# Top-2 mixture of a fused AdaLN-FFN kernel: dense experts with gates, against tiles of scattered token rows with weights at register addresses

## The chip, the cores and the metric

One core of one Trainium2 chip. The metric is device time in microseconds for one execution; lower is better. Three runs of the kernel before gave a median of 1235.52 us (1235.36 to 1236.33).

## The reference, cut to what matters

Two layers on x of 16 x 256 tokens with 256 features (4096 tokens). Layer 0 is a recurrence over 256 steps, then a top-2 mixture of 8 large experts, added to x. Layer 1 conditions x with a shared gated MLP plus a second top-2 mixture of 8 small experts, feeds the result through a quantised FFN and adds it to x. The change touches the second mixture:

```python
def _L1_cond_ref(x, t_emb, router_w, router_t_w, router_bias, sw1, sw3, sw2, rw1, rw2):
    shared_out = jnp.einsum('nh,dh->nd', jax.nn.silu(x_flat @ sw1.T) * (x_flat @ sw3.T), sw2)
    s = jax.nn.sigmoid((x_flat @ router_w.T + t_bias_flat).astype(jnp.float32))
    _, topk_idx = jax.lax.top_k(s + router_bias, TOP_K)
    s_sel = jnp.take_along_axis(s, topk_idx, axis=1)
    gates = jnp.where(denom > EPS, s_sel / (denom + EPS), 1.0 / TOP_K)
    combine = jnp.sum(gates[:, :, None] * jax.nn.one_hot(topk_idx, N_EXPERTS), axis=1)
    H = jax.nn.gelu(jnp.einsum('nd,ehd->enh', x_flat, rw1), approximate=False)   # h = 128
    O = jnp.einsum('enh,edh->end', H, rw2)
    out = (shared_out + jnp.einsum('end,ne->nd', O, combine)) / (N_SHARED + TOP_K)
```

The reference computes all 8 experts for every token and zeroes six of them by `combine`. The FFN behind it needs the largest value of the whole mixture output before it can quantise anything.

## The kernel before, in words

The program runs four stages one behind the other: the recurrence (its token rows are scattered to expert rooms in HBM while it runs), the large experts (39 tiles of 256 token rows, `experts_*`), the mixture (`mixture_pe`, `mixture_act`, `mixture_dve`) and the quantised FFN (`ffn_*`). Each engine has its own instruction stream in a fixed order written out by hand; semaphores tie the streams together. Each fp32 product is made of three f16 products (high by high, high by low, low by high), `split_matmul` (L570 to L573).

The large experts end with scattered adds of their result tiles into `results` in HBM (`store_results`, L1298, from POOL). SyncE then loads `results` back as x1, 512 KB for each group of 512 tokens (`load_x1`, L1467).

The mixture works on 8 groups of 4 x 128 tokens. For a group, ScalarE makes the high half of x (`input_hi`, L668), VectorE the low half (`input_lo`, L734), TensorE transposes both (L605) and ScalarE copies them out of PSUM (`input_T`, L672). TensorE then computes router logits (24 small matmuls), the first layer of the shared MLP (8 units of 6 matmuls with 512 columns), **the first layer of all 8 routed experts** (8 more units like these), the shared second layer (4 units of 12 matmuls with 256 columns) and **the second layer of all 8 experts** (16 units of 2 x 3 matmuls with 256 columns). ScalarE applies tanh or gelu; VectorE finishes the SiLU product (L763, L767), makes low halves (L756), runs the top-2 routing as a chain of small operations (L793 to L807, L775 to L788) and adds each expert's part with its gate as a per-token factor (L836). After each group VectorE takes the largest value (L847, L842); the FFN starts when the last is in (L992).

POOL does nothing in the mixture; its indirect DMAs are in the recurrence (L1268, one row of 1028 bytes for each of 128 partitions, plain write) and in the large experts (L1298, 1024 bytes for each, added to what stands in HBM).

```python
for q2 in range(0, GT, 2):                       # L836, dense: every expert's part of every token
    ...
    dve.scalar_tensor_tensor(y[:, GT * g + q], ps[:, bank_of(...), j * D:(j + 1) * D],
                             comb[:, q, 2 * p + j:2 * p + j + 1], y[:, GT * g + q], ALU.mult, ALU.add)
```

Of the kernel before, what the change touches and what calls it, by code (L numbers as in the profile page):

```python
# [17 lines left out]
P = 128  # L18
# [51 lines left out]
HC = HSC + E  # L70
U_SHARED, U_ROUTED = 1, 1 + 2 * HSC
U_NEXT = U_ROUTED + E
U_OUT = U_NEXT + DC
U_PAIR = U_OUT + GT
UNITS = U_PAIR + GT * E // 2
PRE_UNITS = 1 + DC
YG = GT * (1 + E)
MIX_SCALE = W_SCALE * A_SCALE
LINKS = 24
# [16 lines left out]
def build_program(nc, zT, xn, h0T, WT, b_row, alphaT, gate_wT, gate_b, w1T, b1T, w2T, b2, rwT, rtwT, rbias,  # L96
                  sw1T, sw3T, sw2T, rw1T, rw2T, fw1n, fb1T, fw2n, fb2, const, rows_d, results_d, out):
    ctx = ExitStack()
    with ctx:
# [18 lines left out]
        def carve(a):  # L118
# [3 lines left out]
            def part(n, dt=F32):  # L122
# [10 lines left out]
        hid1_flat = part(2 * HC * GN, F16)  # L133
        hid1 = hid1_flat.rearrange("p (s c n) -> p s c n", s=2, c=HC)
        yqT = hid1_flat[:, 0:DC * N].bitcast(BF16).rearrange("p (k n) -> p k n", k=DC)
        vq_flat = hid1_flat[:, DC * N:].bitcast(U8)
# [3 lines left out]
        xs_flat = part(2 * 2 * DC * GN, F16)  # L140
        xs = xs_flat.rearrange("p (b s k n) -> p b s k n", b=2, s=2, k=DC)
        xsn_flat = part(2 * GT * D, F16)
        xsn = xsn_flat.rearrange("p (s n) -> p s n", s=2)
# [3 lines left out]
        diag = part(DC * P).rearrange("p (c n) -> p c n", c=DC)  # L147
        h0rep = part(DC * P).rearrange("p (c n) -> p c n", c=DC)
        rs2 = part(D)
# [5 lines left out]
        l1w = part(2 * 7168, F16).rearrange("p (s n) -> p s n", s=2)  # L155
        sw1s = l1w[:, :, 0:1024].rearrange("p s (k h) -> p s k h", k=DC)
        sw3s = l1w[:, :, 1024:2048].rearrange("p s (k h) -> p s k h", k=DC)
        sw2s = l1w[:, :, 2048:3072].rearrange("p s (k d) -> p s k d", k=HSC)
        rw1s = l1w[:, :, 3072:5120].rearrange("p s (k h) -> p s k h", k=DC)
        rw2s = l1w[:, :, 5120:7168].rearrange("p s (e d) -> p s e d", e=E)  # L160
        wq_n = part(2 * 2048, BF16).rearrange("p (m n) -> p m n", m=2)
# [29 lines left out]
              for a in (hid.rearrange("p s f n -> p (s f n)"), xs_flat)]  # L191
# [130 lines left out]
        xn_lo = sem("xn_lo")  # L322
        xs_T = sem("xs_T")
        unit = sem("unit")
        sa_used = sem("sa_used")
        tb_ready = sem("tb_ready")
        router_step = sem("router_step")
        ymax_in = sem("ymax_in")
# [1462 lines left out]
```

## Time and profile before

| | us |
|---|---|
| median of three runs | 1235.52 |
| the profiled execution | 1231.89 |
| its span | 1229.8 |
| TensorE busy | 1102.4 (90%) |
| VectorE busy | 898.7 (73%) |
| ScalarE busy | 550.1 (45%) |
| POOL busy | 246.3 (20%) |

The profiled execution is 2.1 us longer than its span (what lies before the first and behind the last instruction) and 3.6 us shorter than the median of the other runs. In the chain that ended last the share of TensorE is 77%, VectorE 10%, ScalarE 8%.

### The profile page before, as it was taken

How to read it: one execution, taken by the hardware profiler on the slowest of the kernel's cores; microseconds unless marked ns; L12 is line 12 of the kernel's file. 1: busy time of each engine (PE TensorE's matmuls, PEld its weight loads, DVE VectorE, ACT ScalarE, POOL GpSimd, SP SyncE). 2: the span in 40 equal slices, each digit the busy share in tenths (PEclk: the TensorE clock that was granted, in tenths of full speed). 3: DMA queues.
4: the chain of work that ended last, by engine and by line, in shares of the span. 5: the costliest groups of instructions: out<-in, count | busy, mean ns of one | idle time of the engine just before them, and what ended most of it. 6: DMA issues, size and time to landing. Idle time of an engine off the chain costs nothing.

```text
span 1229.8 us, 31887 instructions
## 1 busy us (share of the span) xinstructions
PE 1102.4 (90%) x10420; PEld 847.4 (69%) x10421; DVE 898.7 (73%) x3007; ACT 550.1 (45%) x1743; POOL 246.3 (20%) x285
## 2 busy tenths in 40 slices
PE   6777777877878999999999999789999999996898
PEld 5665665665657888888888888646776567763355
DVE  5676676776776688965555555468898988988887
ACT  4555555555554333333333333362445424444276
POOL 1002112112115675243333333300000000001000
PEclk9999999999999999999999999989999999998999
DMA  7222332332334577444444444241000000000024
GB/s 179 78 71 86 100 94 85 100 98 81 99 96 113 94 168 141 88 73 61 63 62 63 64 64 64 50 124 69 2 1 1 0 1 1 1 1 1 1 34 105
DMA packets 98711, 82.31 MB, mean 67 GB/s; under 512 B 58529, under 2 KB 88354, under 8 KB 98594
## 3 DMA queue, kind: packets, MB, share of 16 engines
q1 hardware_dynamic: 82946, 57.98, 18.6%
q0 software_dynamic: 15648, 22.86, 10.7%
q8 instruction: 62, 1.02, 0.3%
q14 instruction: 55, 0.45, 0.1%
HBM read 41.18 MB, written 33.60 MB: 61 GB/s over the span
## 4 chain that ended last, share of the span: by engine, by line
PE 77%; DVE 10%; ACT 8%; issue 3%; DMA 1%; SPq 0%; POOL 0%; DVEq 0%
PE ps L572 24%; PE ps L1129 17%; PE ps L1139 17%; PE ps L1686 7%; DVE ps L1615 6%; PE ps L1691 4%; ACT work L1539 4%; ACT ps L1534 3%; DVE imax L1008 2%; PE ps L1656 2%; PE ps L917 1%; PE ps L922 1%; PE ps L888 1%; PE ps L1664 1%; DVE W L836 1%
## 5 line engine op out<-in xcount | busy, mean ns | idle before, releaser
L1157 ACT ACTIVATE lane<-ps,b_now 128x256 f32<-128x256 f32 x312 | 147.7, 474 | 260.0 <-PE ps L1129 246.0
L1129 PE MATMUL ps<-lane,W 128*128 128x256 f16 x1872 | 212.8, 274 | 0.9 <-issue 0.8
L1139 PE MATMUL ps<-W,lane 128*128 x1872 | 210.9, 273 | 0.2
L1129 PEld LDWEIGHTS ps<-lane,W 128*128 x1872 | 183.7, 98 | 23.8 <-issue 1.7
L1139 PEld LDWEIGHTS ps<-W,lane 128*128 128x128 f16 x1872 | 182.6, 98 | 22.3 <-issue 0.8
L1686 PE MATMUL ps<-work 128*128 128x16 f16 x2048 | 98.9, 177 | 86.1 <-ACT work L1539 85.5
L1686 PEld LDWEIGHTS ps<-work 128*128 128x128 f16 x2048 | 76.2, 107 | 137.8 <-ACT work L1539 136.4
L572 PE MATMUL ps<-W,work 128*128 128x512 f16 x768 | 168.5, 381 | 0.1
L1298 POOL DMA_INDIRECT results<-lane,dest x78 | 124.7, 1598 | 217.0 <-DVE lane L1212 184.3
L1224 DVE TENSOR_TENSOR lane<-lane 128x256 f16<-128x256 f32 x312 | 133.3, 427 | 10.8
L572 PEld LDWEIGHTS ps<-W,work 128*128 128x128 f16 x768 | 74.8, 98 | 90.1 <-issue 1.9
L572 PE MATMUL ps<-work,W 128*128 128x256 f16 x1152 | 127.4, 273 | 0.0
L572 PEld LDWEIGHTS ps<-work,W 128*128 128x128 f16 x1152 | 112.2, 98 | 13.7 <-ACT W L672 0.6
L1222 DVE CAST lane<-lane 128x256 f16<-128x256 f32 x312 | 92.8, 298 | 20.6 <-ACT lane L1157 20.6
L1212 DVE SCALAR_TENSOR_TENSOR lane<-ps,b_now 128x512 f32<-128x512 f32 x39 | 26.9, 691 | 110.7 <-PE ps L1139 110.7
L1629 DVE TENSOR_TENSOR work<-ps,work 128x32 f16<-128x32 f32 x256 | 48.9, 191 | 78.4 <-ACT ps L1541 78.1
L1656 PE MATMUL ps<-work 128*128 128x128 f32 x256 | 98.3, 490 | 5.8 <-DVE work L1579 4.9
L836 DVE SCALAR_TENSOR_TENSOR W<-ps,comb,W 128x256 f32 (+1 forms) x256 | 101.6, 474 | 2.0 <-PE ps L572 1.9
L1615 DVE TENSOR_TENSOR_SCAN ps<-ps,work 128x64 f32<-128x64 f32 x256 | 76.4, 298 | 30.9 <-ACT ps L1534 8.2
L1268 POOL DMA_INDIRECT rows<-work,slot_of x64 | 63.1, 985 | 156.5 <-DVE ps L1615 152.6
L1598 DVE SCALAR_TENSOR_TENSOR work<-ps,alpha,work 128x16 f32<-128x16 f32 x510 | 93.3, 225 | 0.0
L1534 ACT ACTIVATE ps<-ps 128x32 f32<-128x32 f32 x256 | 46.6, 182 | 94.8 <-PE ps L1691 94.8
(213 smaller groups left out, 1466.7 us busy)
## 6 DMA issues: line engine op xcount, KB each, us to landing
stage<-in_w1T SPq DMA_DIRECT2D x16, 512.0 KB, 3.6
stage<-in_w2T SPq DMA_DIRECT2D x16, 512.0 KB, 4.1
b_now<-in_b SPq DMA_DIRECT2D x39, 128.0 KB
work<-in_zT SPq DMA_DIRECT2D x32, 128.0 KB, 2.1
results<-in_xn SPq DMA_DIRECT2D x32, 128.0 KB
W<-results SPq DMA_DIRECT2D x8, 512.0 KB, 3.8
rows<-work SPq DMA_DIRECT2D x8, 257.0 KB, 5.2
out<-W SPq DMA_DIRECT2D x4, 512.0 KB, 4.0
```

What stands on the lines that cost most here:

```text
L572: last = pe.matmul(dst, lhs(a, k), rhs(b, k), start=(n == 0 and k == ks[0]), stop=(n == 2 and k == ks[-1]))
L836: dve.scalar_tensor_tensor(y[:, GT * g + q], ps[:, bank_of(U_PAIR + GT * p + q), j * D:(j + 1) * D], comb[:, q, 2 * p + j:2 * p + j + 1], ...
L1129: last = pe.matmul(ps[:, f % 4, 0:ST], of_e(W1[:, bass.ds(e, 1), a, k, f * P:(f + 1) * P]), xT[:, p, b, k], start=(i == 0 and k == 0), sto ...
L1139: last = pe.matmul(ps[:, 4 + q, 0:D], hid[:, a, f, q * P:(q + 1) * P], of_e(W2[:, bass.ds(e, 1), b, f]), start=(i == 0 and f == 0), stop=( ...
L1157: act.activation(v4[:, f % 4], ps[:, f % 4, 0:ST], ACT.Relu, bias=b1_now[:, p, f:f + 1], scale=A_SCALE / W_SCALE).then_inc(l1_v, 1)
L1222: dve.tensor_copy(hid[:, 0, f], v4[:, f % 4]).then_inc(split0, 1)
L1224: dve.tensor_tensor(hid[:, 1, f], v4[:, f % 4], hid[:, 0, f], ALU.subtract).then_inc(l1_hid, 1)
L1298: pool.indirect_dma_start(out=results_d, in_=obuf[:, p, q], in_offset=None, compute_op=ALU.add, out_offset=bass.IndirectOffsetOnAxis(ap=de ...
L1598: dve.scalar_tensor_tensor(zs[:, j % 2, c // BATCH, k, :, 1], h[:, k], alpha[:, k:k + 1], z[:, j, k, c:c + BATCH], ALU.mult, ALU.add).then ...
L1615: dve.tensor_tensor_scan(ps[:, 5, 0:2 * DB], ps[:, 6, 0:2 * DB], zs[:, j % 2, s % STEPS_PER_TILE].rearrange("p c b v -> p (c b v)"), 0.0, ...
L1656: pe.matmul(dst, wz[:, k, cols], z[:, slot, k, :], start=(k == 0), stop=False, skip_group_check=True)
L1686: pe.matmul(ps[:, b + m, c:c + BATCH], w[:, k, m * P:(m + 1) * P], hring[:, prev, 0, k, pc:pc + BATCH], start=False, stop=False, skip_grou ...
```

## The change

The routed experts of the second mixture are no longer computed for all tokens. In order:

- **Routing and scatter.** Two groups are routed at once (`PAIR` = 8 tiles of 128 tokens, 32 chained operations, `mix_route_op`), in 4 steps. TensorE counts ranks (`mix_ranks`) so that every token gets a slot in a room of its expert. POOL scatters each group's rows (high and low halves of x, token number and gates: `MROW` = 260 words, 1040 bytes) to `mrows` in HBM, 8 indirect DMAs a group, 64 in all (`mixture_pool`). The rows wait in 4 buffers (`XBUFS`). While this runs, TensorE and VectorE work on the shared MLP, 8 units a step (32 of 96), and 12 units more after the last step.
- **Table.** VectorE makes a table of 39 tiles of 256 slots (`mix_table`), SyncE writes padding behind every expert's last row and loads the tiles, 3 buffers (`TILE_BUFS`).
- **Tiles.** For each of 39 tiles: TensorE transposes it (8 transposes), 6 matmuls of 256 columns, gelu, high and low halves, 6 matmuls of 256 columns; both layers read the expert's weights at an address from a register. VectorE multiplies by the gate (`tile_out`) into `mout`, and POOL scatters the tile's two halves, plain writes of 1024 bytes a row, to `mresults` in HBM at `mdest`. 30 shared units are spread over the tiles; 22 follow.
- **Combine.** When the last tile has landed, SyncE loads `mresults` (1 MB a group, two results a token); VectorE adds them to the shared part and takes the group's largest value.

PSUM: the units have 3 banks in turn where they had 8. At the start 8 unused rooms of `mrows` are filled from an input (2.1 MB, HBM to HBM). Cut to its core:

```diff
+TAIL = 4
+MROW = D + TAIL
+XBUFS = 4
+PAIR = 2 * GT
+STEPS_M = GROUPS // 2
+TILE_BUFS = 3
+MIX_OPS = 32
+UNITS = 2 * HSC + GT
+STEP_UNITS = 8
+BRIDGE_UNITS = 12
+TILE_UNITS = 30
+LATE = 6
+COMBINE = (0, 1, 2, 6, 3, 4, 5, 7)
...
         def mixture_act(act):
             def input_hi(g):
...
+                if g >= XBUFS:
+                    act.wait_ge(moved[b], 2 * GT * 16 * (g // XBUFS))
+                act.activation(xsn[:, b, :, 0:D], x1[:, GT * g:GT * g + GT], ACT.Copy, scale=A_SCALE).then_inc(xn_hi, 1)
...
+            def tile_gates(n):
+                b = n % TILE_BUFS
+                tail = lambda k: mrow[:, b, :, D + k:D + k + 1]
+                mine = mtile_f[:, 0, n]
+                dve.wait_ge(mrow_in[b], 16 * (n // TILE_BUFS) + 16)
+                if n >= TILE_BUFS:
+                    dve.wait_ge(mstored[b], SQ * 16 * (n // TILE_BUFS))
+                dve.scalar_tensor_tensor(mdest[:, b], tail(1), mine, tail(0), ALU.is_equal, ALU.add).then_inc(mdest_set, 1)
+                dve.scalar_tensor_tensor(mmask[:, b], tail(1), mine, tail(3), ALU.is_equal, ALU.mult).then_inc(mgate_step, 1)
+                dve.wait_ge(mgate_step, 2 * n + 1)
+                dve.tensor_tensor(mgate[:, b], mmask[:, b], tail(2), ALU.add).then_inc(mgate_step, 1)
...
+            for n in range(SLOT_TILES):
+                tile_lo(n)
+                for v in tile_units(n):
+                    shared(v)
+                if n < SLOT_TILES - 1:
+                    tile_gates(n + 1)
+                if n:
+                    tile_out(n - 1)
+            tile_out(SLOT_TILES - 1)
+
+            def combine(at):
+                g, b = COMBINE[at], at % TILE_BUFS
+                yg = y[:, GT * g:GT * g + GT]
+                if g < LATE:
+                    dve.wait_ge(routed_in[b], 16 * (at // TILE_BUFS) + 16)
+                    link(dve, dve.tensor_tensor(yg, yg, routed[b][:, :, 0], ALU.add))
+                else:
+                    dve.wait_ge(unit_read, output_unit(g, GT - 1) + 1)
+                link(dve, dve.tensor_tensor(yg, yg, routed[b][:, :, 1], ALU.add))
+                dve.tensor_reduce(ymax[:, g:g + 1], yg.rearrange("p q d -> p (q d)"), AX.X, ALU.max).then_inc(combined, 1)
...
+        def mixture_pool(pool):
+            rows_flat = mrows_d.rearrange("r s n -> (r s) n")
+            for g in range(GROUPS):
+                pool.wait_ge(router_step, MIX_OPS * (g // 2 + 1))
+                pool.wait_ge(xn_lo, g + 1)
+                pool.wait_ge(tok_set, g + 1)
+                for k in range(2):
+                    for q in range(GT):
+                        at = GT * (g % XBUFS) + q
+                        pool.indirect_dma_start(out=rows_flat, in_=xrow[:, g % XBUFS, q], in_offset=None,
+                                                out_offset=bass.IndirectOffsetOnAxis(ap=mslot_of[:, k, at:at + 1], axis=0))\
+                            .then_inc(moved[g % XBUFS], 16)
+            for n in range(SLOT_TILES):
+                b = n % TILE_BUFS
+                pool.wait_ge(mout_set, n + 1)
+                pool.wait_ge(mdest_set, n + 1)
+                for q in range(SQ):
+                    pool.indirect_dma_start(out=mresults_d, in_=mout[:, b, q], in_offset=None,
+                                            out_offset=bass.IndirectOffsetOnAxis(ap=mdest[:, b, q], axis=0))\
+                        .then_inc(mstored[b], 16)
```

The last combines stand on VectorE as follows: 8 units, combine 0 to 2, the 4 output units of group 6, combine 3, then three times 2 units and a combine (4, 5, 6), the 4 output units of group 7, combine 7.

The order of VectorE's work in the tile stage of the change, tiles 4 and 5 of the loop; `mdest`, `mmask` and `mgate` are the three operations of `tile_gates` (L1039 to L1042), L1053 is `tile_out`, L1046 `tile_lo`, L985 the read of a shared output unit:

```order
L1053 TENSOR_TENSOR lane<-ps,mgate 128x512 [waits mgate_step,m2_ps]
L1046 SCALAR_TENSOR_TENSOR lane<-work,lane 128x256 [waits mhi]
L985 TENSOR_SCALAR W<-ps 128x256 [waits unit]
L1039 SCALAR_TENSOR_TENSOR mdest<-stage,mtile_f 128x2 [waits mstored1,mrow_in1]
L1040 SCALAR_TENSOR_TENSOR mmask<-stage,mtile_f 128x2
L1042 TENSOR_TENSOR mgate<-mmask,stage 128x2 [waits mgate_step]
L1053 TENSOR_TENSOR lane<-ps,mgate 128x512 [waits mgate_step,m2_ps]
L1046 SCALAR_TENSOR_TENSOR lane<-work,lane 128x256 [waits mhi]
L1039 SCALAR_TENSOR_TENSOR mdest<-stage,mtile_f 128x2 [waits mstored2,mrow_in2]
```

Here the wait for a tile's scattered results (`mstored`) stands between one `tile_out` and the next; before the change VectorE waited in this stage for TensorE, ScalarE and itself.

POOL's queue in the change, from the last row scatter to the first result scatters:

```order
L1328 DMA mrows<-W,mslot_of 36864x260 [waits tok_set,xn_lo,router_step]
L1328 DMA mrows<-W,mslot_of 36864x260 x7
L1336 DMA mresults<-lane,mdest 16384x256 [waits mdest_set,mout_set]
L1336 DMA mresults<-lane,mdest 16384x256
L1336 DMA mresults<-lane,mdest 16384x256 [waits mdest_set,mout_set]
```

Before the change POOL's queue goes from its last L1298 straight to the FFN's work; 64 + 78 indirect DMAs now stand between.

## Rows read from the trace of the kernel before

**Rows 1.** The page: span, and the chain that ended last by line.

```profile
span 1229.8 us, 31887 instructions
...
PE ps L572 24%; PE ps L1129 17%; PE ps L1139 17%; PE ps L1686 7%; DVE ps L1615 6%; PE ps L1691 4%; ACT work L1539 4%; ACT ps L1534 3%; DVE imax L1008 2%; PE ps L1656 2%; PE ps L917 1%; PE ps L922 1%; PE ps L888 1%; PE ps L1664 1%; DVE W L836 1%
```

**Rows 2.** Busy time by stage: the mixture and its first 10 us.

```profile
795.00:1115.00 320.00, 307.21 (x2241) 200.97 (x2242) 270.83 (x666) 132.54 (x227) 0.64 (x2) 0.98 0.07 21
...
795.00:805.00 10.00, 2.23 (x23) 1.74 (x23) 1.23 (x1) 4.28 (x5) 0.64 (x2) 0.66 0.42 117
```

**Rows 3.** The chain of waits in the mixture: start, us, what.

```profile
904.53 37.04 PE ps L572 x264
...
959.03 20.89 PE ps L572 x96
...
1113.69 0.70 DVE ymax L842
```

**Rows 4.** The timeline of the mixture: start, us, engine, line.

```profile
800.23 1.06 ACT L668 ACTIVATE W<-W 128x1024 f16<-128x1024 f32 x1 [4.04 <-DMA W<-results]
...
801.34 1.03 PE L605 MATMUL ps<-identh,W 128*128 128x128 f16 x8 [7.68 <-ACT W L668]
...
804.84 0.78 PE L572 MATMUL ps<-rw_s,W 128*128 128x8 f16 x24 [1.21 <-ACT W L672]
...
805.66 0.19 DVE L793 SCALAR_TENSOR_TENSOR r_sel<-ps,t_bias 128x32 f32<-128x32 f32 x1 [3.12 <-PE ps L572]
...
1093.95 15.88 PE L572 MATMUL ps<-work,W 128*128 128x256 f16 x144
```

**Rows 5.** Groups of instructions by line and form: busy, mean ns | idle before.

```profile
L1157 ACT ACTIVATE lane<-ps,b_now 128x256 f32<-128x256 f32 x312 | 147.7, 474 | 260.0 <-PE ps L1129 246.0 <-DVE lane L1224 9.1 <-issue 0.3
L1224 DVE TENSOR_TENSOR lane<-lane 128x256 f16<-128x256 f32 x312 | 133.3, 427 | 10.8
L836 DVE SCALAR_TENSOR_TENSOR W<-ps,comb,W 128x256 f32 x192 | 76.1, 473 | 1.2 <-PE ps L572 1.1
L767 DVE SCALAR_TENSOR_TENSOR W<-ps,W 128x512 f32<-128x512 f32 x32 | 22.1, 691 | 3.3
L672 ACT ACTIVATE W<-ps 128x1024 f16<-128x1024 f16 x16 | 15.5, 1019 | 1.4 <-PE ps L605 1.4
L825 DVE TENSOR_SCALAR W<-ps 128x256 f32 x24 | 8.6, 414 | 0.8 <-PE ps L572 0.8
L1045 DVE TENSOR_TENSOR W<-W 128x1024 f32<-128x1024 f32 x4 | 4.6, 1216 | 0.0
L803 DVE TENSOR_TENSOR r_t<-r_t,prio 128x32 f32<-128x32 f32 x16 | 3.1, 192 | 0.5
L779 DVE TENSOR_SCALAR r_k<-r_m 128x4 f32<-128x4 f32 x8 | 1.3, 162 | 0.0
L710 ACT ACT_TABLE_LOAD x1 | 1.3, 1283 | 0.0
```

**Rows 6.** The timeline of POOL: scattered rows one behind the other.

```profile
381.07 0.96 POOL L1268 DMA_INDIRECT rows<-work,slot_of  x1 [0.30 <-issue]
382.34 0.97 POOL L1268 DMA_INDIRECT rows<-work,slot_of  x1 [0.30 <-issue]
```

**Rows 7.** L1268 asked for by line: from its start to its landing.

```profile
DMA to landing us min/median/max: 2.4/3.0/4.5
```

**Rows 8.** The timeline around the last results of the large experts.

```profile
779.55 0.69 DVE L1212 SCALAR_TENSOR_TENSOR lane<-ps,b_now 128x512 f32<-128x512 f32 x1 [3.56 <-PE ps L1139]
...
780.52 1.55 POOL L1298 DMA_INDIRECT results<-lane,dest  x1 [6.29 <-DVE lane L1212]
...
782.38 1.55 POOL L1298 DMA_INDIRECT results<-lane,dest  x1 [0.30 <-issue]
...
792.86 1.55 POOL L1298 DMA_INDIRECT results<-lane,dest  x1 [0.30 <-issue]
...
796.52 8.51 SPq L1467 DMA_DIRECT2D W<-results  x3
```

**Rows 9.** DMA issues: KB each, median us to landing.

```profile
W<-results SPq DMA_DIRECT2D x8, 512.0 KB, 3.8
```

More of the change, by code:

```diff
@@ new lines, in router @@
+            def router(g):
+                pe.wait_ge(xs_T, 2 * g + 2)
+                if g >= 2 and g % 2 == 0:
+                    pe.wait_ge(router_step, MIX_OPS * (g // 2 - 1) + 1)
+                for q in range(GT):
+                    at = (GT * (g % 2) + q) * E
+                    last = split_matmul(ps[:, 2, at:at + E], lambda s, k: xs[:, g, s, k, q * P:(q + 1) * P],
+                                        lambda s, k: rw_s[:, s, k], range(DC))
+                last.then_inc(rt_ps, 1)
@@ new lines, in mix_ranks @@
+            def mix_ranks(m):
+                flat = m16_m[:].rearrange("p j e -> p (j e)")
+                pe.wait_ge(router_step, MIX_OPS * m + 15)
+                pe.matmul(MIX_RANKS, tri[:], flat, start=True, stop=False, skip_group_check=True)
+                for j in range(PAIR):
+                    last = pe.matmul(MIX_RANKS[:, (j + 1) * E:], ones16[:],
+                                     m16_m[:, j:j + 1].broadcast_to([P, PAIR - j, E]),
+                                     start=False, stop=(j == PAIR - 1), skip_group_check=True)
+                last.then_inc(rank_ps, 1)
@@ L663, in mixture_pe @@
-            mix_groups(pe, mix)
+            for g in range(2):
+                transposes(g)
+            pe.wait_ge(tb_ready, 1)
+            pe.wait_ge(wt_cp, 4)
+            pe.wait_ge(m16_zero, 1)
+            for m in range(STEPS_M):
+                v = STEP_UNITS * m
+                for g in (2 * m, 2 * m + 1):
+                    router(g)
+                for k in range(3):
+                    shared(v + k)
+                mix_ranks(m)
+                for k in range(3, 6):
+                    shared(v + k)
+                for g in (2 * m + 2, 2 * m + 3):
+                    if g < GROUPS:
+                        transposes(g)
+                    shared(v + 4 + g - 2 * m)
@@ new lines, in mixture_pe @@
+            pe.wait_ge(mtable, 1)
+            tile_transposes(0)
+            ex = None
+            for n in range(SLOT_TILES):
+                if n < SLOT_TILES - 1:
+                    tile_transposes(n + 1)
+                ahead = tile_first(n)
+                for v in tile_units(n):
+                    shared(v)
+                if n:
+                    tile_second(n - 1, ex)
+                ex = ahead
+            tile_second(SLOT_TILES - 1, ex)
+            for v in range(TAIL_UNIT, UNITS * GROUPS):
+                shared(v)
@@ new lines, in mixture_dve @@
+            first_late, last_late = output_unit(LATE, 0), output_unit(GROUPS - 1, 0)
+            for v in range(TAIL_UNIT, first_late):
+                shared(v)
+            for at in range(3):
+                combine(at)
+            for v in range(first_late, first_late + GT):
+                shared(v)
+            combine(3)
+            for n in range(3):
+                for v in range(first_late + GT + 2 * n, first_late + GT + 2 * n + 2):
+                    shared(v)
+                combine(4 + n)
@@ L853, in ffn_groups @@
+            for v in range(last_late, UNITS * GROUPS):
+                shared(v)
+            combine(GROUPS - 1)
         def ffn_groups(eng, group):
@@ L1513, in _ @@
             experts_pool(pool)
+            mixture_pool(pool)
             ffn_pool(pool)
```

751 lines of the change are left out of this document (460 added, 291 removed).

## The prediction

> **What bounds the kernel now.** I read the page first: one TensorE line, L572, carries 24% of the chain that ended last [rows 1]. It is the mixture's matmul helper, so the mixture is the largest piece of the path after the two layers of the large experts. The stage table then says how: in 320 us of mixture TensorE is busy 307.2, VectorE 270.8, ScalarE 132.5 and POOL 0.6 [rows 2]. The chain of waits shows nothing but TensorE for whole groups: 37.04 us for 264 matmuls [rows 3], plus 0.9 us of transposes. So the mixture is bound by TensorE, with VectorE some 12% behind it, and POOL and the DMA (7% busy) stand free. The piece ends with the last maximum at 1113.69 + 0.70 = 1114.4 [rows 3]; the 115.4 us behind it are the FFN, which the change leaves alone.
>
> **What the change takes off TensorE.** A 512-column matmul costs 20.89 / 96 = 0.218 us [rows 3], one of 256 columns 15.88 / 144 = 0.110 [rows 4]. Per group the routed experts lose 48 x 0.218 + 96 x 0.110 = 21.0 us of the 37.9, 168 us over 8 groups. Each of 39 tiles adds 12 x 0.110 and 8 transposes of 0.056 (half the 1.03 us of eight at the lower clock [rows 4]), 1.77 us, 69 us in all. TensorE's work falls by 99 us. If TensorE stayed the bound, that would be the gain. I think it does not stay the bound, and go through the new path piece by piece.
>
> **1. To the first slots.** x1 lands at 800.23 and VectorE reads the first logits at 805.66 [rows 4]. Now two groups have to be transposed and routed first: two more ScalarE copies of 1.02 [rows 5] and 24 more router matmuls, 0.78 [rows 4]: 808.4. Then 31 chained operations. Small ones take 0.16 to 0.19 [rows 5]; with the handover and a few twice as wide I take 0.21, 6.5 us. Five unit operations of 0.69 stand between them, 3.4, and about 3 us go into the first unit and its tanh. The slots stand at 821.3.
>
> **2. 64 row scatters on POOL.** The nearest row is L1268, a plain scatter of 1028 bytes a partition: its starts are 382.34 - 381.07 = 1.27 us apart when nothing holds it [rows 6], the landing is 3.0 us from the start (2.4 to 4.5) [rows 7]. I take 1.26: 63 x 1.26 + 3.0 = 82.4, from 821.3 to 903.7. Meanwhile VectorE needs per step 32 x 0.21 + 3 x 3 x 0.69 + 4 x 0.41 + 2 x 1.22 = 17 us [rows 5], under POOL's 16 x 1.26 = 20.2, and TensorE about 14. So this stretch is POOL's, and the shared units, the table and the bridge units are hidden in it (all done near 900). The four row buffers bite: group 7 can only be rounded once group 3 has landed, about 864, its slots come near 880, and POOL wants them at 882. The cover is 2 us thin; if it is gone, a few us are lost.
>
> **3. First tile.** A tile is 266 KB; 512 KB land in 3.8 us [rows 9], I take 3.2. Then transposes, copy 1.02, transposes and first layer 1.1, the one table load of gelu 1.28, gelu 0.47, halves 0.8, second layer 0.66, `tile_out` 0.69 [rows 5] and handovers of 0.2 each: 8.2. First `tile_out` done: 915.1.
>
> **4. The tile loop.** This term decides. In VectorE's order the wait for `mstored` of tile n - 3 stands directly ahead of `tile_out` of tile n - 2. So every `tile_out` from tile 1 on waits until the results of the tile just before it have landed in HBM. The three buffers overlap nothing: `mdest` is rewritten two tiles too early. One round is: `tile_out` to POOL's start 0.28 (779.55 + 0.69 to 780.52) [rows 8]; the second scatter starts 1.26 later [rows 6] and lands 3.0 after that [rows 7]; three small operations 0.16 each with one handover, 0.55; `tile_out` 0.69 plus 0.03 [rows 5, 8]. **5.81 us a tile.** TensorE wants 1.77 + 0.77 units of 1.31 = 2.8, ScalarE 1.02 + 0.47 + 0.4 + 0.3 = 2.2, VectorE 2.3: all wait. There are 36 such rounds (tiles 1 to 36): 209.2 us, to 1124.3.
>
> What bounds it: a landing of 2.4 gives 5.21 [rows 7]. If the plain scatter costs what the adding one does (starts 1.86 apart; the last starts at 792.86 and SyncE goes on at 796.52, 3.6 later [rows 8]) a round is 7.0. The new scatter is plain and as wide as L1268, so I stay with 5.81. The Trainium skill (DMA: Bandwidth & Descriptors, Anatomy of one DMA) puts a DMA issued from POOL at about 2.0 us plus bytes / 436e3, an estimate of 2.3 us for these 131 KB. By it a round would be 5.1 and the sum 25 us lower; the trace's 3.0 disagrees and is used.
>
> **5. Landing the last three tiles.** They follow each other on POOL: 0.28 + 5 x 1.26 + 3.0 = 9.6, to 1133.9. Eight shared units fit beside it.
>
> **6. Loading and combining.** 1 MB: between 3.8 and twice that [rows 9]; I take 5.4: 1139.3. Then VectorE: two adds and a maximum of 1024 values, 1.22 each [rows 5], for six groups 22.0; one add and a maximum for two, 4.9; 8 output units of 0.47 [rows 5], 3.8; three pairs of first-layer units, 9 x 0.69 = 6.2. Group 7's output units need a low half that VectorE makes only then, so TensorE's 4 x 1.31 is exposed, +4.7. Together 41.6, loads hidden behind it from the second on. End 1180.9.
>
> **Sum.** The mixture ends at 1180.9 where it ended at 1114.4: **+66.5 us**. On the profiled execution that is 1231.89 + 66.5 = 1298.4; its like of the median, 3.6 higher, is 1235.52 + 66.5 = **1302.0**. Free of cost I count the 2.1 MB copy at the start: the recurrence waits for other engines and not for DMA after its first 10 us; bound +3 us.
>
> **Rivals.**
> - *The tile loop runs at TensorE's pace.* If the stores came back within the 2.8 us that TensorE needs, 36 x 3.0 = 108 us would fall away: 1194, faster than before. The point at which it decides: the round must be under 5.81 - 66.5 / 36 = 3.96 us. For it speaks that the DMA is idle here. Against: without any landing time, 0.28 + 1.26 + 0.96 + 0.55 + 0.72 = 3.77 us stand in the round already, so the landing would have to follow POOL within 0.2 us, and the shortest of 64 was 2.4 - 0.96 = 1.4 us behind it [rows 6, 7]. It could only be that the order is not what I read. 4%.
> - *The plain result scatter is as dear as the adding one.* 36 x 1.17 + 3.6 = +46 us: 1348. For it: the same 1024 bytes from the same kind of tile; against: L1268 differs from it by 4 bytes a row and writes plainly too. 10%.
> - *TensorE falls to its lower clock in the loop.* In the first 10 us of the mixture, after 7.7 us of idling, the granted clock was 0.66, and eight transposes took 1.03 us [rows 2, 4]. In the loop TensorE would work 2.8 us and idle 3.0. At 1.2 GHz a tile is 5.6 us of work, still under 5.81, but its handovers (some 0.9) are then in the way: 6.5 a round, +25 us, 1327. 14%. The Trainium skill (TensorE: Matmul & The Clock Gate, HAM oscillation — how this bites in real kernels) tells of just this, bursts shorter than the waits between them, with every burst starting at the lower clock; it is the rule that speaks against this change, and rows of a 320 us stage at 0.98 cannot show it.
> - *Landings are quick.* 2.4 us everywhere: 36 x 0.6 and some, 1278. It is the low side of the forecast.
>
> **How the numbers follow.** Forecast with both its sides 72%, higher rivals 24%, the faster one 4%. The range runs from the quick landing with 10 us off my estimated terms (1278 - 13 = 1265) to the dear scatter (1348): 1265 to 1348. A measurement here tells about 0.2%, 2.5 us, from no change. No case lands near zero: slower 0.95, same 0.01, faster 0.04.
>
> **What would show it.** In the profile after: POOL's L1328 64 times, 1.26 apart, nearly without gaps; VectorE's longest wait in total at L1039, released by the DMA to `mresults`, about 3.3 us for each of 36; L1053 every 5.8 us; TensorE about half busy between 915 and 1124. If L1039 waits little and L1053 stands 2.8 to 3 us apart, step 4 is wrong and the kernel is faster. If the rounds are 5.8 but the end is not near 1298, steps 1 to 3 or 6 are.

## The result and the profile after

| | before | changed |
|---|---|---|
| median of four runs, us | 1235.92 (1235.36 to 1236.65) | 1340.49 (1338.51 to 1343.26) |
| ratio | | 1.0847, 95% interval 1.0826 to 1.0869 |
| profiled execution, its span | | 1341.17, 1339.3 |

The change makes the kernel 8.5% slower (4.7% when the same kernel ran again, run 9 below); the forecast was 1302.0 with a range of 1265 to 1348. The direction is right and the time lies inside the range, 38.5 us above the forecast. As it turns out below, two terms missed in opposite directions, and the larger miss is not a property of the code alone.

The page of the changed kernel, its head and the chain that ended last (against [rows 1]):

```profile
span 1339.3 us, 31036 instructions
PE 1071.3 (80%) x10084; PEld 812.9 (61%) x10085; DVE 823.0 (61%) x2840; ACT 552.0 (41%) x1736; POOL 388.2 (29%) x428
PE 51%; issue 15%; DVE 15%; ACT 8%; POOL 5%; another core or an unknown queue 3%; DMA 2%; SPq 0%; DVEq 0%; POOLq 0%; ACTq 0%
```

TensorE's share of the chain fell from 77% to 51%. Its busy time fell by 31 us and not by the 99 that I counted, mostly since it worked at a lower clock: in the whole mixture stage it is busy for 275.2 us at a granted clock of 0.82 (799 to 1224 us), and for 230.8 us at 0.90 in run 10 below, with the same matmuls (795 to 1088 us). The busy time of the three new stages (against [rows 2]), columns as there: start and end, length, then PE, PEld, DVE, ACT and POOL busy, granted clock, DMA share, GB/s. They are the row scatters, the tile loop and the combining:

```profile
825.00:950.00 125.00, 70.39 (x523) 41.44 (x523) 54.02 (x159) 27.95 (x45) 64.62 (x64) 0.75 0.24 83
955.00:1165.00 210.00, 150.83 (x1064) 94.86 (x1063) 82.25 (x242) 85.26 (x142) 70.87 (x73) 0.88 0.31 96
1170.00:1225.00 55.00, 31.25 (x166) 18.15 (x164) 42.05 (x53) 7.44 (x13) 3.19 (x3) 0.81 0.43 158
```

In the first stage no engine is busy for more than 57% of the time, in the second TensorE for 72% and no other for more than 41%: in both, the time goes in waits of one engine for another or for a landing. What the engines waited for from 795 to 1240 us (engine, line, released by: us in total, times, longest):

```profile
POOL mresults L1336 <- DVE lane L1053: 133.3, 38, 24.2
DVE mdest L1039 <- DMA mresults<-lane,mdest: 117.2, 36, 4.3
...
POOL mrows L1328 <- DVE mslot_of L931: 69.4, 4, 27.7
...
DVE W L867 <- remote: 35.3, 3, 13.7
ACT W L814 <- DVE W L867: 31.0, 3, 14.9
```

**The loop.** L1039 waits 36 times, 117.2 / 36 = 3.26 us each, for the landing of the tile just before. The timeline shows one round (start, us, engine, line):

```profile
984.94 0.69 DVE L1053 TENSOR_TENSOR lane<-ps,mgate 128x512 f32<-128x512 f32 x1
985.54 0.41 DVE L1046 SCALAR_TENSOR_TENSOR lane<-work,lane 128x256 f16<-128x256 f32 x1
985.90 0.97 POOL L1336 DMA_INDIRECT mresults<-lane,mdest  x1 [3.00 <-DVE lane L1053]
987.18 0.98 POOL L1336 DMA_INDIRECT mresults<-lane,mdest  x1 [0.30 <-issue]
...
989.70 0.22 DVE L1039 SCALAR_TENSOR_TENSOR mdest<-stage,mtile_f 128x2 uint32<-128x2 f32 x1 [3.73 <-DMA mresults<-lane,mdest]
...
990.16 0.69 DVE L1053 TENSOR_TENSOR lane<-ps,mgate 128x512 f32<-128x512 f32 x1
```

0.96 + 1.28 + 2.52 + 0.46 = 5.22 us: `tile_out` and handover, the second scatter, its landing, the three gate operations. That is step 4 with a landing of 2.52 instead of 3.0, and 0.09 less for the gate operations.

**The row scatters.** L1328 is where I was wrong. POOL does not run without gaps. It waits 69.4 us for slots; 27.7 of them are the first wait, the others are 13 to 15 us each. The steps' slots, which I expected to keep pace with POOL's 20.2 us, are 34.7, 34.4 and 35.3 us apart (the timeline of VectorE):

```profile
824.75 0.17 DVE L931 CAST mslot_of<-slot_m 128x16 uint32<-128x16 f32 x1
859.43 0.17 DVE L931 CAST mslot_of<-slot_m 128x16 uint32<-128x16 f32 x1
893.86 0.17 DVE L931 CAST mslot_of<-slot_m 128x16 uint32<-128x16 f32 x1
929.17 0.17 DVE L931 CAST mslot_of<-slot_m 128x16 uint32<-128x16 f32 x1
```

What holds them up stands in no step of mine. POOL's first run of 16 scatters goes from 825.4 to 846.5. The timeline of its second half:

```profile
835.75 0.25 PE L638 MATMUL ps<-rw_s,W 128*128 128x8 f16 x4 [0.54 <-issue]
836.46 0.17 PE L638 MATMUL ps<-rw_s,W 128*128 128x8 f16 x1 [0.46 <-issue]
836.57 0.97 POOL L1328 DMA_INDIRECT mrows<-W,mslot_of  x1 [0.31 <-issue]
837.18 0.18 PE L638 MATMUL ps<-rw_s,W 128*128 128x8 f16 x1 [0.55 <-issue]
...
845.50 0.97 POOL L1328 DMA_INDIRECT mrows<-W,mslot_of  x1 [0.30 <-issue]
848.56 0.23 DVE L867 SCALAR_TENSOR_TENSOR W<-ps,t_bias 128x64 f32<-128x64 f32 x1 [13.75 <-remote]
848.82 0.26 ACT L814 ACTIVATE W<-W 128x64 f32<-128x64 f32 x1 [14.93 <-DVE W L867]
```

TensorE ends the router logits at 837.4. VectorE's L867 waits for them and for nothing else that is still to come, and starts at 848.56, 11 us later, when POOL's run is over. The profile finds no releaser and writes "remote". Near the same time TensorE's small matmuls get gaps of half a microsecond with nothing to wait for. Waits on "remote" of 6 to 14 us stand in all four runs of 16 scatters, so the slots of steps 2 to 4 come some 14 us late. Three of the five end 2 to 3 us behind the run's last scatter, the other two (at 877.3 and 905.7) inside the run. I call it the hold-up.

It is in this trace once before, where the recurrence ends with 7 scatters in a row (376.6 to 385.2). ScalarE stands still there for 3.7 us, up to the end of the last of them; the same place in the trace of before, and in run 9 below, has no such wait (VectorE's 3 us wait some microseconds earlier is in all of them). The timeline of the first result:

```profile
384.20 0.96 POOL L1539 DMA_INDIRECT rows<-work,slot_of  x1 [0.30 <-issue]
385.08 0.47 ACT L1420 ACTIVATE lane<-ps,b_now 128x256 f32<-128x256 f32 x1 [3.67 <-PE ps L1392]
```

The kernel before has the same scatters and the same instructions there. So this wait tells of any run in the study whether the hold-up was there, also of one without row scatters in the mixture.

### The profile page after: what moved, and what is told of

Read it like the earlier page. It is cut to its first block, busy times and chain, and to the rows that moved or that the text cites. A ratio compares the mean times of both kernels' runs of the same rounds, so it can differ in the third digit from the quotient of the medians.

```text
span 1339.3 us, 31036 instructions
## 1 busy us (share of the span) xinstructions
PE 1071.3 (80%) x10084; PEld 812.9 (61%) x10085; DVE 823.0 (61%) x2840; ACT 552.0 (41%) x1736; POOL 388.2 (29%) x428
## 4 chain that ended last, share of the span: by engine, by line
PE 51%; issue 15%; DVE 15%; ACT 8%; POOL 5%; another core or an unknown queue 3%; DMA 2%; SPq 0%; DVEq 0%; POOLq 0%; ACTq 0%
PE ps L1392 14%; PE ps L1402 14%; PE ps L1994 7%; POOL mresults L1336 5%; DVE ps L1923 4%; PE ps L638 4%; PE ps L1999 4%; ACT work L1847 3%; ACT ps L1842 3%; DVE imax L1250 2%; PE ps L1964 1%; PE ps L1159 1%; PE ps L1164 1%; PE ps L1130 1%
## 5 line engine op out<-in xcount | busy, mean ns | idle before, releaser
L1336 POOL DMA_INDIRECT mresults<-lane,mdest x78 | 75.7, 971 | 145.5 <-DVE lane L1053 133.3
L638 PE MATMUL ps<-W,work 128*128 128x512 f16 x384 | 107.6, 435 | 12.1 <-DVE W L985 8.1
L1493 DVE CAST lane<-lane 128x256 f16<-128x256 f32 x312 | 93.7, 300 | 24.0 <-ACT lane L1420 20.7
L1328 POOL DMA_INDIRECT mrows<-W,mslot_of x64 | 64.6, 1010 | 87.7 <-DVE mslot_of L931 69.4
L638 PE MATMUL ps<-work,W 128*128 128x256 f16 x384 | 60.2, 322 | 34.3 <-DVE W L973 20.3
L1847 ACT ACTIVATE work<-ps 128x32 f16<-128x32 f32 x256 | 50.6, 198 | 75.2 <-DVE ps L1923 64.0
```

Source lines behind the costliest of these rows:

```text
L638: last = pe.matmul(dst, lhs(a, k), rhs(b, k), start=(n == 0 and k == ks[0]), stop=(n == 2 and k == ks[-1]))
L1336: pool.indirect_dma_start(out=mresults_d, in_=mout[:, b, q], in_offset=None, out_offset=bass.IndirectOffsetOnAxis(ap=mdest[:, b, q], axis=0))\
L1493: dve.tensor_copy(hid[:, 0, f], v4[:, f % 4]).then_inc(split0, 1)
```

## The experiments

Theory B, formed from this trace: scatters that follow each other on POOL hold up what the other engines signal to each other. Rivals: the steps are slow by themselves, or the bytes do it. Theory A is my step 4: the order of the store wait alone makes the loop 5.2 us. The unedited kernel's line numbers hold unless a line says otherwise.

### 1. Stores three tiles deep

```diff
-        mdest = sb("mdest", [P, TILE_BUFS, SQ, 1], U32)
+        mdest = sb("mdest", [P, 2 * TILE_BUFS, SQ, 1], U32)
...
-                if n >= TILE_BUFS:
-                    dve.wait_ge(mstored[b], SQ * 16 * (n // TILE_BUFS))
-                dve.scalar_tensor_tensor(mdest[:, b], tail(1), mine, tail(0), ALU.is_equal, ALU.add).then_inc(mdest_set, 1)
+                dve.scalar_tensor_tensor(mdest[:, n % (2 * TILE_BUFS)], tail(1), mine, tail(0), ALU.is_equal, ALU.add).then_inc(mdest_set, 1)
...
                 dve.wait_ge(mgate_step, 2 * n + 2)
+                if n >= TILE_BUFS:
+                    dve.wait_ge(mstored[b], SQ * 16 * (n // TILE_BUFS))
                 dve.tensor_tensor(mout[:, b], ...
```

> Edit: mdest gets 6 buffers instead of 3, and the wait for the stores of tile n - 3 moves from the gate operations of tile n (ahead of tile_out of tile n - 1 or earlier) to tile_out of tile n, which really overwrites mout; up to three tiles' stores are now under way. Theory A (the loop is 5.24 us a tile because each tile_out waits for the landing of the tile just before it): the wait at L1039 disappears, the loop falls to the next bound, TensorE's 2.8 us or POOL's two scatters of 1.27 with a handover, 2.6 to 2.9 us a tile, so 36 x 2.4 = 85 us less: 1340 - 85 = 1255. Theory B (row scatters that follow each other on POOL hold up the semaphore updates of all engines, as seen in the row-scatter stretch): POOL now runs nearly without a pause in the loop, updates come late there too, and the spacing stays above 3.5 us; total between 1275 and 1330. If the store wait was not the bound of the loop at all, nothing moves.

Measured: 1283.64 us (1272.35 to 1284.79; three of four executions above 1283), 1.0341 times before [1.0294, 1.0388]. The unedited kernel was not among the runs taken together with this one (runs 1 to 4); its first result is of another set. The wait at `mdest` is gone and the loop fell, but to 3.60 us a tile (39 `tile_out` from 972.1 to 1108.8), not to 2.6 to 2.9. Of the waits from 975 to 1100:

```profile
POOL mresults L1336 <- DVE lane L1053: 41.1, 19, 5.3
...
ACT lane L832 <- remote: 29.6, 8, 5.9
```

The hold-up is now in the loop too: ScalarE waits eight times, up to 5.9 us, for something that the profile cannot name. Theory A would explain the fall, and theory B what is left above 2.8 us; runs 9 and 10 test both.

### 2. A pause after every 8 row scatters

```diff
+                if g:
+                    pool.wait_ge(moved[(g - 1) % XBUFS], 2 * GT * 16 * ((g - 1) // XBUFS + 1))
                 for k in range(2):
                     for q in range(GT):
```

> Edit: POOL waits until the 8 row scatters of a group have landed before it issues the next group's. Theory B (runs of back-to-back scatters delay the other engines' semaphore updates from some 8 us after the run starts until it ends, and so the next step's slots come 10 to 14 us late): a run is now 8 scatters, 10 us, so updates are late by at most 2 or 3 us, the slots of steps 1 to 3 come 8 to 12 us earlier, and though POOL loses 8 x 2 us in waits, the last row scatter starts at about 925 where it started at 949: total 1310 to 1325. Rival (POOL's own pace and VectorE's chain set the stretch, the late updates are an effect of something else, such as VectorE's queue): four more waits inside steps make every step 2 to 3 us longer, last scatter at 955 to 965, total 1345 to 1355.

Measured: 1311.72 us (1309.13 to 1315.44), 1.0591 [1.0574, 1.0609]. The slots are 26.4, 25.1 and 27.4 us apart, where run 1 of the same set has 34.3, 35.3 and 33.6. L867's remote waits have shrunk from 35.3 in the first result to 9.6 us, all waits on "remote" together from 53.2 to 22.7. More waiting on POOL made the kernel 29 us faster than its first result.

### 3. No row scatters

```diff
-                        pool.indirect_dma_start(out=rows_flat, in_=xrow[:, g % XBUFS, q], in_offset=None, ...
+                    pool.memset(idle[:], 0.0).then_inc(idled, 1)
...
-                sp.dma_start(mrow[:, b], mrows_d[bass.ds(r, 1)]...
+                sp.dma_start(mrow[:, b], pads_d[n % 16:n % 16 + 1]...
```

> Left out: the 64 row scatters (POOL writes an unused buffer with memsets instead and signals the group as moved), the tiles are loaded from the padding input instead of the scattered rows, and the results go to destinations made from constants. All other instructions and waits stand. Theory B (scatters hold up the updates): no unit update or router result is seen late, a step takes VectorE its 17 us, so the table stands near 821 + 3 x 17 + some = 880 to 890 where it stood at about 960, the loop stays at 5.2 us a tile; total 1340 - 70 = 1265 to 1280. Rival (steps are slow because of TensorE or VectorE themselves, 31 us each whatever POOL does): table near 950, total above 1330.

Measured: 1287.42 us, 1.0407 [1.039, 1.0425], 7 above the expected 1265 to 1280. No wait on "remote" is left anywhere. The slots are 20.1, 20.3 and 19.1 us apart and the table stands at 892.7. The rival is out: without the scatters a step takes 19 to 20 us. VectorE is busy for 14.2 to 15.3 us of each, so the rest is the handovers of its chain with TensorE and ScalarE.

One more reading makes this comparison safe. The hold-up was there in this very execution, at the 7 scatters that end the recurrence, which the edit leaves alone:

```profile
385.48 0.96 POOL L1543 DMA_INDIRECT rows<-work,slot_of  x1 [0.30 <-issue]
386.37 0.47 ACT L1424 ACTIVATE lane<-ps,b_now 128x256 f32<-128x256 f32 x1 [3.66 <-PE ps L1396]
```

The same wait is 3.65 to 3.69 us long in runs 1, 2 and 4 too. So runs 3 and 4 met the same occasion as runs 1 and 2, and it is the edit that took the hold-up out of their mixture.

### 4. The same bytes by plain DMAs

```diff
-                        pool.indirect_dma_start(out=rows_flat, in_=xrow[:, g % XBUFS, q], in_offset=None, ...
+                        r = P * (8 * g + 4 * k + q)
+                        sp.dma_start(rows_plain[r:r + P], xrow[:, g % XBUFS, q]).then_inc(moved[g % XBUFS], 16)
```

> Left out: the 64 row scatters of POOL; SyncE writes the same rows with 64 plain DMAs of the same 133 KB each to fixed rows instead, so they do not go to their slots, and the tiles are loaded from the padding input; results go to destinations made from constants. The padding writes wait for these DMAs. Theory B in the form that POOL's software-made descriptors are what holds up the other engines: no late updates, slots early, as without any row write, total 1270 to 1285. Rival C (the bytes do it: 8.5 MB in 1040-byte rows into HBM keep the DMA rings busy that also carry the updates): updates as late as with POOL's scatters, table near 950, total above 1320.

Measured: 1291.90 us, 1.0436 [1.0418, 1.0453], 7 above the expected 1270 to 1285. Slots 21.3, 20.5 and 20.7 us apart, table at 894.1, no "remote" wait. The same rows through SyncE's plain DMAs hold up nobody. It is not the bytes; here it takes POOL's indirect DMAs. Whether plain DMAs issued by POOL would do the same was not tried.

### 5 to 8. Four variants, and a surprise common to all

Four more runs on one chip: a pause after every 4 row scatters; a 64-word memset between two of them; on top of the three-deep version, plain stores of the results by SyncE; and on top of it a landing wait on POOL before every second tile.

Run 5, ahead of each 4 row scatters:

```diff
                 for k in range(2):
+                    if g or k:
+                        h = g if k else g - 1
+                        pool.wait_ge(moved[h % XBUFS], 2 * GT * 16 * (h // XBUFS) + (GT * 16 if k else 2 * GT * 16))
```

Run 6, behind each row scatter:

```diff
+                        if g + k + q:
+                            pool.wait_ge(idled, 8 * g + GT * k + q)
+                        pool.memset(idle[:, 0:64], 0.0).then_inc(idled, 1)
```

Run 7, in SyncE's loop over the tiles, in place of POOL's result scatters:

```diff
                 load_tile(n)
+                if n >= 3:
+                    store_tile(n - 3)
```

Run 8, ahead of a tile's result scatters:

```diff
+                if n and n % 2 == 0:
+                    pool.wait_ge(mstored[(n - 1) % TILE_BUFS], SQ * 16 * ((n - 1) // TILE_BUFS + 1))
```

> Edit: POOL waits for the landing of the row scatters after every 4, not after every 8 (one of the waits stands inside a group). Hold-up theory: runs of 4 scatters, 5.1 us, are shorter than the 7 to 9 us after which the other engines' updates come late, so no wait of another engine shows a late update in the stretch; but each landing wait costs POOL 2.3 to 3 us (measured in the run with pauses after 8), so a step of 16 scatters takes 16 x 1.27 + 4 x 2.0 = 28 to 31 us: no longer set by the late slots but by POOL. Slots 28 to 31 us apart, total 1310 to 1335, between the pause after 8 and no pause. Rival (the hold-up is proportional to the number of scatters and not to their runs): late updates stay, total 1340 or more.

> Edit: after each row scatter POOL writes 64 unused words a partition (a memset, 0.1 to 0.2 us), so that the scatters are some 1.45 to 1.55 us apart instead of 1.27, with no wait for a landing. If POOL's density of scatters decides (what they bring per us is a little more than can be taken beside the other engines' updates): the late updates disappear or shrink to below 3 us, a step takes 16 x 1.5 = 24 us, total 1340 - 3 x 10 = 1300 to 1312. If the number of scatters issued without waiting for a landing decides: updates as late as before, each step some 3 us longer, total 1345 to 1355.

> Edit on top of the version whose stores are three tiles deep (1283.6 us, a tile_out every 3.60 us). Left out: POOL's 78 result scatters; SyncE stores each tile's two halves with plain DMAs to fixed rows instead, so the results do not go to their tokens. Same bytes, same waits. Hold-up theory: the 3.60 us are TensorE's pace plus updates held up by POOL's scatters; without them a tile takes 2.8 to 3.0 us, and the late updates in the loop disappear: 1284 - 38 x 0.7 = 1257, between 1250 and 1265. Rival (3.60 us is the chain through the engines, with TensorE's clock and its handovers, or the loads): spacing and total stay, 1278 to 1290.

> Edit on top of the version whose stores are three tiles deep (1283.6 us): POOL waits for the landing of the last result scatter before every second tile, so never more than 4 scatters follow each other. Hold-up theory: 4 x 1.27 plus a landing wait of about 1.5 us is 6.6 us for two tiles, 3.3 a tile, and no update is late: 1284 - 38 x 0.3 = 1272, between 1265 and 1280. Rival (no hold-up in the loop, POOL's wait only adds): 3.8 to 4.2 us a tile, 1290 to 1305.

| | us | ratio |
|---|---|---|
| 5, pause after 4 | 1320.90 | 1.0725 [1.0702, 1.0748] |
| 6, memset between | 1292.21 | 1.0491 [1.0467, 1.0516] |
| 7, deep, results plain | 1294.34 | 1.0513 [1.0486, 1.0541] |
| 8, deep, wait every 2 tiles | 1237.50 | 1.0044 [1.002, 1.0068] |

Only run 5 came out inside one of its expected ranges. Runs 6 and 8 were faster than any case that I had allowed, and run 7 was slower.

Run 6 looks like a proof that spacing the scatters cures the hold-up. It is none. Its scatters are 1.30 us apart instead of 1.27, for the 0.17 us memset only filled the 0.30 us that lie between two scatters anyway:

```profile
829.33 0.97 POOL L1330 DMA_INDIRECT mrows<-W,mslot_of  x1 [0.16 <-issue]
830.31 0.17 POOL L1335 MEMSET idle<- 128x64 f32 x1
830.63 0.97 POOL L1330 DMA_INDIRECT mrows<-W,mslot_of  x1 [0.16 <-issue]
```

And runs 7 and 8, whose row scatters are those of the changed kernel, show no hold-up either: run 8's slots are 21.7, 21.9 and 19.6 us apart where run 1's, from the same code, were 34.3, 35.3 and 33.6. Nor has any of the four traces ScalarE's 3.7 us wait at the end of the recurrence, which no edit touches. So these four say nothing of the hold-up; it was not there to be cured. What run 5 does show is the price of its pauses: POOL waits 31.0 us in 13 landings, and the slots are 21.7, 28.8 and 26.8 us apart. Run 7 is inconclusive in another way. I put SyncE's stores between its loads of the tiles, so the tiles came late (from 975 to 1100, TensorE waited for them 13 times, up to 5.2 us), and a tile took 5.2 us:

```profile
PE ps L723 <- DMA stage<-mrows: 35.5, 13, 5.2
```

### 9 and 10. The changed kernel and the three-deep one again, side by side

> The changed kernel itself, nothing edited. Why: in the last four runs the row-scatter stretch showed no late updates even where its code was that of the changed kernel (slots 21.7, 21.9, 19.6 us apart where they had stood 34.3, 35.3, 33.6 apart), so the comparison of runs from different chips is not safe. Theory D (the hold-up of semaphore updates by back-to-back scatters is there on one chip and not, or weaker, on another): where it is absent, slots 19 to 22 us apart, table near 891, total 1340 - 45 = 1290 to 1297, as with the spaced scatters (1292), whose spacing then did nothing. Where it is present, 1338 to 1343 as before. Rival (it hangs on the program, and the unedited one always has it): 1338 to 1343 on any chip.

> The version whose stores are three tiles deep, unedited, beside the changed kernel on the same chip. On a chip without the hold-up: the loop falls from 5.24 to TensorE's and POOL's 2.8 to 3.0 us a tile (3.60 with the hold-up; 3.56 where POOL paused for a landing every two tiles), so 38 x 2.3 = 87 us under the changed kernel of the same chip: 1292 - 87 = 1205, faster than the kernel before. On a chip with the hold-up: 1272 to 1285 as measured. Rival (another bound at 3.5 us, whatever the hold-up): 1230 to 1240 without the hold-up.

Measured: the changed kernel **1290.64 us** (1288.14 to 1293.71), 1.047 [1.0453, 1.0488]; the three-deep one **1204.51 us** (1203.06 to 1206.13), 0.9763 [0.9747, 0.9779], faster than the kernel before. The changed kernel is 50 us below its first result without one edit. It has no "remote" wait, and L867 follows the router matmuls at once while POOL scatters just as densely:

```profile
828.58 0.96 POOL L1328 DMA_INDIRECT mrows<-W,mslot_of  x1 [0.30 <-issue]
828.81 1.35 PE L638 MATMUL ps<-rw_s,W 128*128 128x8 f16 x48
829.85 0.97 POOL L1328 DMA_INDIRECT mrows<-W,mslot_of  x1 [0.30 <-issue]
830.20 0.23 DVE L867 SCALAR_TENSOR_TENSOR W<-ps,t_bias 128x64 f32<-128x64 f32 x1 [0.43 <-PE ps L638]
```

Its loop is the same as in the first result, a round of 5.22 us (the store wait does not care about the hold-up):

```profile
985.95 0.69 DVE L1053 TENSOR_TENSOR lane<-ps,mgate 128x512 f32<-128x512 f32 x1
986.91 0.97 POOL L1336 DMA_INDIRECT mresults<-lane,mdest  x1 [2.98 <-DVE lane L1053]
988.19 0.97 POOL L1336 DMA_INDIRECT mresults<-lane,mdest  x1 [0.31 <-issue]
990.70 0.22 DVE L1039 SCALAR_TENSOR_TENSOR mdest<-stage,mtile_f 128x2 uint32<-128x2 f32 x1 [2.54 <-DMA mresults<-lane,mdest]
991.17 0.69 DVE L1053 TENSOR_TENSOR lane<-ps,mgate 128x512 f32<-128x512 f32 x1
```

In the three-deep version a tile takes 2.83 us (922.6 to 1030.0), TensorE is busy for 101.3 of 105 us in the loop, and the granted clock is 1.00:

```profile
925.00:1030.00 105.00, 101.32 (x947) 80.30 (x945) 72.74 (x214) 70.13 (x123) 71.28 (x73) 1.00 0.60 177
```

The two kernels ran in one set and differ in this wait and the three more buffers of `mdest` that it needs. So the order of one wait is worth 86 us where nothing else disturbs, and run 1's 3.60 us a tile was 0.77 above it. Run 8, which seemed a cure (the loop at 3.56 us), in truth costs 33 us against this version (1237.5 and 1204.5, from two sets in which the kernel before ran at 1232.4 and 1233.6).

### 11 and 12. Versions meant to bear the hold-up

The three-deep version with a 192-word memset after every scatter, and with the pause after every 8 row scatters.

> Edit on top of the three-deep version: after every row scatter and every result scatter POOL writes 192 unused words a partition, so scatters stand about 1.42 us apart instead of 1.27 (the 64-word memset of the earlier spaced run took 0.17 us, but its scatters were 1.30 apart, since it filled the 0.30 us that lie between two scatters anyway). On a chip without the hold-up: POOL is nearly continuous from the slots on, so the stretch gets 64 x 0.15 = 10 us longer at most, and a tile 2 x 1.42 = 2.84 to 3.1 us where it took 2.83: 1205 + 10 to 20 = 1212 to 1225. On a chip with it: if density decides, updates come late by less and the total is clearly under the 1284 of the unspaced version, 1225 to 1255; if not, 1290.

> Edit on top of the three-deep version: POOL waits for a group's landing before the next group's row scatters. On a chip without the hold-up: 7 waits of 1.2 to 2.3 us less what POOL idled for slots anyway, so 1205 + 8 to 15 = 1213 to 1220. On a chip with it: the stretch gains the 29 us that the same edit gained there alone, 1284 - 29 = 1255.

Measured: 1213.61 us, 0.984 [0.9824, 0.9856], and 1221.55 us, 0.9913 [0.9888, 0.9938]. Neither showed the hold-up, so only the price of the remedies was measured, 9 and 17 us beside run 10, the first as expected, the second 2 us above; the fastest version of the study is the plain three-deep one. These two runs and the first four were on the same chip. On the first visit to it the pause-after-8 edit still waited 22.7 us on "remote", on the last not at all. So "one chip has it, another not" (theory D) falls too, in that form: it comes and goes with the occasion.

## Why the prediction was right or wrong, step by step

The same milestones, in us of each profiled execution. "First result" has the hold-up, run 9 is the same kernel without it.

| step | predicted | first result | run 9 |
|---|---|---|---|
| SyncE starts loading x1 | 796.5 | 799.9 | 795.8 |
| 1, first slots ready | 821.3 | 824.9 | 820.8 |
| 2, row scatters landed (first tile load) | 903.7 | 956.5 | 908.9 |
| 3, first `tile_out` done | 915.1 | 974.0 | 923.3 |
| 4, 36 rounds | 209.2 | 189.6 | 188.7 |
| 5, last stores landed | 9.6 | 9.2 | 9.1 |
| 6, load and combine | 47.0 | 51.1 | 50.5 |
| mixture ends | 1180.9 | 1223.8 | 1171.7 |

1. **First slots** were right: 25 us after the loads start, in both.
2. **The row scatters** are the step that failed: 131.6 us where I had 82.4. I wrote that the stretch is POOL's, since VectorE needs 17 us a step and TensorE 14, both under POOL's 20.2. Without the hold-up that holds: slots 21.3, 21.7 and 19.2 us apart, VectorE busy for 14 to 16 us of each (no more than my 17), POOL waiting 0.7 us for the second and third slots together. The stretch is 88.1 us there, and the 6 us too many are nearly all POOL's own: its scatters are 1.34 us apart on average and not 1.26. Most take 0.97 us, but 11 of the 64 take more than 1.00, up to 1.89. All 11 start while VectorE makes a low half (L968 or L973, a scaled difference of two tiles in SBUF, written as f16), and all six that start during an L968 are among them. The timeline of run 9:

```profile
841.33 0.97 POOL L1328 DMA_INDIRECT mrows<-W,mslot_of  x1 [0.30 <-issue]
842.44 1.22 DVE L968 SCALAR_TENSOR_TENSOR W<-W 128x1024 f16<-128x1024 f32 x1
842.60 1.89 POOL L1328 DMA_INDIRECT mrows<-W,mslot_of  x1 [0.30 <-DVE mslot_of L931]
```

With the hold-up the slots come 14 us late three times, which is most of the 49 us. The prediction has no term for it: it took the engines as independent of POOL while they signal to each other. The trace of before gave no sign either: its run of 7 scatters at the end of the recurrence (376.0 to 384.8) holds up nothing.
3. **First tile**: from the first tile load to the first `tile_out` done 14.4 us in run 9 and 17.5 in the first result, where I had 11.4.
4. **The tile loop**: the mechanism was right to the wait. The term was mis-sized by its landing, 2.5 us where I took the 3.0 median of [rows 7]. 36 rounds of 5.24 are 188.7 in place of 209.2. The Trainium skill (DMA: Bandwidth & Descriptors, Anatomy of one DMA) gave an estimate of 2.3 us and a round of 5.1; the trace's landing plus wake-up of 2.52 lies between the skill's estimate and mine, nearer to the former, and so does the round.
5. **Last stores**: right.
6. **Combining**: 4 us short. VectorE waits for TensorE's output units (L991) for 9.3 us in the first result and 8.3 in run 9, where I had 4.7. The loads are hidden as I said: VectorE waits 0.3 us for the first 1 MB in the first result, and never in run 9.

The errors have opposite signs: in the first result 49 us too little in step 2 and 20 too much in step 4. The total was inside the range, but not for the reason that I gave for its upper end: that was luck. Run 9, without the hold-up, is inside it too, 11 us under the forecast, and there the 20 us of step 4 are the largest error.

**The rivals.** The loop at TensorE's pace was rejected for the right reason, the order of the wait; changing the order brought just that pace, 2.83 us against the 2.8 in step 4, and 1204.5 for the whole where the rival said 1194. The dear scatter is out: 1.27 us apart, 2.5 to land. Quick landings are what happened. The lower clock is there in part: the granted clock over the loop is 0.88, so some of it runs at 1.2 GHz and most at 2.4, and a matmul takes TensorE 150.83 / 1064 = 0.142 us there where it took 101.32 / 947 = 0.107 in run 10. It costs nothing on the path of the loop, since the round of 5.22 us adds up from POOL, the landing and VectorE alone. The Trainium skill (TensorE: Matmul & The Clock Gate, HAM oscillation — how this bites in real kernels) says that bursts shorter than the waits between them start at the lower clock. That is not what this trace has. TensorE is busy for 2.4 to 5.1 us of each round, no gap between its matmuls is longer than 2.1 us (984 to 1160 us), and yet the granted clock of a round lies anywhere from 0.52 to 1.00, as in these two rounds, one behind the other (busy time by stage, columns as above):

```profile
1042.36:1047.58 5.22, 3.39 (x25) 1.75 (x23) 2.03 (x7) 3.25 (x6) 1.94 (x2) 1.00 0.32 101
1047.58:1052.80 5.22, 3.48 (x20) 2.36 (x21) 2.63 (x8) 1.37 (x2) 1.94 (x2) 0.52 0.34 101
```

**What stays open.** What the hold-up is. Shown: within one set of four runs on one chip it is there with POOL's indirect row scatters (run 1), less with a pause after every 8 (run 2), and absent from the mixture when they are left out or replaced by plain DMAs of the same bytes (runs 3 and 4), though all four traces have it at the end of the recurrence; the four timed runs of the first result agree within 0.4%. Also shown: in eight later runs it did not appear, among them the unedited kernel. The kernel before ran at a median of 1237.4 us beside runs 1 to 4 and at 1232.4 to 1233.6 beside the eight (1235.9 beside the first result). In the first result and runs 1 to 4 SyncE starts loading x1 at 799.9 to 801.9, in the eight at 795.7 to 797.7. Most of this difference, 3 us, is the wait at the end of the recurrence, where POOL scatters 7 in a row; that the same wait makes the kernel before slower in those sets is likely, but it was not traced there. Which condition of the chip brings it, and whether spacing or the number of scatters in a row decides, was not settled: the runs that asked this met no hold-up.

## What to carry to other kernels

Where buffers come in threes, ask in which order the consumer waits for them: a wait that guards one small buffer but stands ahead of the previous tile's last operation turns three buffers into one, here 5.24 us a tile instead of 2.83. A variant that gains is compared with its unedited parent in the same set of runs; run 6 and run 8 would each have been told as a cure. A piece of the program that no edit touches, here the 7 scatters at the end of the recurrence, tells whether two traces were taken under the same condition. And a stretch in which POOL scatters without a pause while the other engines signal each other often should be counted with a price of tens of microseconds that may or may not be paid.

## What the runs showed of the hardware that was not expected

- On some occasions work that is ready waits while POOL issues indirect scatters back to back: VectorE up to 13.75 us on "remote" beside a run of 16, ScalarE 3.7 us beside a run of 7, TensorE's matmuls with gaps of 0.5 us from 10 us into the first run of 16. It cost this kernel 50 us (1340.5 against 1290.6). The same 8.5 MB written by SyncE's plain DMAs cost nothing of the kind.
- Two indirect scatters of 128 rows of 1 KB are 1.27 us apart on POOL, of which 0.30 is idle; a memset of 0.17 us fits into that gap at a cost of 0.03. From start to landing the median is 2.6 us for the row scatters and 2.4 for the result scatters of run 9, and 3.0 for those of the recurrence before.
- A scatter that POOL starts while VectorE makes a low half from SBUF to SBUF (L968, 1.22 us) takes up to 1.89 us instead of 0.97, longer the more of VectorE's instruction is still to come (842.60 in run 9, with 1.06 us to come; 822.58, with 0.57 to come, takes 1.43).
- The granted clock is 1.00 over the loop of run 10, where TensorE is busy for 96% of the time, and 0.88 over that of the first result, with the same matmuls in 72% of it. In rounds of 5.22 us it falls as low as 0.52 with no gap in TensorE's work longer than 2.1 us.
